# Starting the expert loop of a routed feed-forward layer on tables of the first half of the tokens

## The chip, the core and the metric

The kernel runs on one core of a Trainium2 chip. The metric is the time of one execution on the device, in microseconds (us). A core has five engines with their own instruction streams: TensorE (PE in the profile; PEld is its weight load), VectorE (DVE), ScalarE (ACT), GpSimd (POOL) and SyncE (SP), which here only starts transfers. Engines wait for each other through semaphores; each engine works its own stream strictly in the order written.

## What is computed

The reference is a stack of six sub-layers over 4096 tokens of width 128: routed feed-forward, causal attention, routed feed-forward again with the same weights, a second feed-forward, a two-branch attention, the second feed-forward again. Only the routed one matters here. It is computed twice, as `x = x + 0.5 * ffn(layernorm(x))` with

```python
logits = jnp.einsum('blh,he->ble', x, Wr) + br
top_expert = jnp.argmax(logits, axis=-1)
mask = jax.nn.one_hot(top_expert, 4, dtype=x.dtype)
for e in range(4):
    h1 = jax.nn.relu(jnp.einsum('blh,hf->blf', x, We1[e]) + be1[e])   # 128 -> 512
    oe = jnp.einsum('blf,fh->blh', h1, We2[e]) + be2[e]               # 512 -> 128
    out = out + mask[..., e:e + 1] * oe
```

So each token needs one expert of four.

## The kernel before, in words

`route_experts` is one such sub-layer; it is called with n = 0 (call 1, at the start of the kernel) and n = 1 (call 2, after the causal attention). It has two phases.

Routing. The 4096 tokens are 32 tiles of 128, in G = 8 groups of 4. DVE walks a software pipeline over steps s = 0 to 10: `statistics(s)`, `locate(s - 3)`, `scales(s)`, `choose(s - 2)`. ACT normalises, PE transposes a group (`turn`), computes its logits (`route`), and, once `choose` has made the one-hot mask, counts the ranks of the tokens within their experts (`tally`, into one of two halves of the PSUM tile `pos`, by the parity of the group). `locate` turns ranks into row numbers (`place`). POOL then scatters the normalised rows, one indirect transfer per tile of 128 tokens (32 per call), into a table in HBM, `routed_rows`, which has one region per expert. This is called the input scatter below.

Expert loop. The rows of each expert are cut into tiles of 128; at most SLOTS0 = 32 + 4 - 1 = 35 tiles (slots) occur. After the last group DVE computes from the final counts a table `tab`: for each slot its first row in `routed_rows` and the offset of its expert's weights. SP writes zero rows (`pad`) behind the end of each expert's rows, waits for the table, the pads and all 32 scatters (`sent`), and then loads the 35 row tiles into a ring of R = 12 buffers. For each slot PE transposes the rows (`turn_row`), ACT and DVE split them into two f16 parts (`high_x`, `low_x`), DVE copies the expert's weights into a ring of 6 buffers (`weights`), PE computes the hidden layer (`hidden`, 16 matmuls), ACT and DVE split the result (`relu`, `low`), PE computes the output (`output`, 13 matmuls), ACT copies it to a ring of S buffers (`result`), and POOL scatters it back to its tokens' places (the output scatter, 35 per call). POOL's queue has the output scatters behind the input scatters. A load into a buffer of the row ring waits until the output scatter of the slot 12 before has returned; `result` waits for the scatter S slots before.

In call 1 the weights come in f32 and are split into f16 parts on the way: `start.high` on ACT, `start.low` on DVE. Pairs 0 and 1 and the bias belong to this sub-layer; pairs 2, 3 and 4 belong to the second feed-forward layer, which runs much later.

Of the kernel before, what the change touches and what calls it, by code (L numbers as in the profile page):

```python
# [11 lines left out]
ALU = mybir.AluOpType  # L12
ACT = mybir.ActivationFunctionType
AX = mybir.AxisListType

P = 128
# [3 lines left out]
NT = TOK // P  # L20
# [5 lines left out]
E0, F0 = 4, 512  # L26
# [10 lines left out]
REGION = TOK + P  # L37
SLOTS0 = NT + E0 - 1
PADS = E0 + SLOTS0 - NT
ROWS = E0 * REGION + (SLOTS0 - NT) * P  # L40
REC = D + 1
FW = 5 * F0 + D
# [407 lines left out]
def route_experts(nc, tag, X, XNT, ident, rank, w, weights_in, consts, f0w, rows_d, y_d, tab, sent, returned, n,  # L450
                  start=None, ident_in=None):


    G = 8
    GT = NT // G
    wr, br, pick, tri, base, first, steps, numbers = (*w, *consts)
    R, S, W = 12, len(returned), 6
    with ExitStack() as ctx:
# [25 lines left out]
        expert = m.sb("expert", [P, SLOTS0])  # L484
        ones = m.sb("ones", [P, P], BF16)
# [32 lines left out]
        with nc.Block() as block:  # L518

            @block.vector  # L520
            def _(dve):
# [59 lines left out]

                for s in range(G + 3):
# [11 lines left out]
                link = Chain(dve, table)  # L594
# [4 lines left out]
                link(nc.vector.tensor_copy(ends[:, 0:1], tiles_of[:, 0:1]))  # L599
                for e in range(1, E0):  # L600
                    link(nc.vector.tensor_tensor(ends[:, e:e + 1], ends[:, e - 1:e], tiles_of[:, e:e + 1], ALU.add))
                link(nc.vector.tensor_scalar(jump[:], tiles_of[:], -float(P), float(REGION), ALU.mult, ALU.add))
                link(nc.vector.tensor_tensor(past[:], numbers[:].unsqueeze(2).broadcast_to([P, SLOTS0, E0]),
                                             ends[:].unsqueeze(1).broadcast_to([P, SLOTS0, E0]), ALU.is_ge))
                link(nc.vector.tensor_tensor(shift[:], past[:], jump[:].unsqueeze(1).broadcast_to([P, SLOTS0, E0]),
                                             ALU.mult))
                link(nc.vector.tensor_reduce(row[:], shift[:], AX.X, ALU.add))
                link(nc.vector.tensor_reduce(expert[:], past[:, :, 0:E0 - 1], AX.X, ALU.add))
                nc.vector.scalar_tensor_tensor(tab[:, 0, :], numbers[:], float(P), row[:], ALU.mult, ALU.add)\
                    .then_inc(tab_ready, 1)  # L610
                nc.vector.tensor_scalar(tab[:, 1, :], expert[:], float(FW), None, ALU.mult).then_inc(tab_ready, 1)
                dve.wait_ge(tab_ready, 2)
# [70 lines left out]
            @block.sync  # L683
            def _(sp):
                if start:
                    start.load(sp)
                sp.wait_ge(pad_ready, 2)
                sp.dma_start(rows_d[E0 * REGION:, :].rearrange("(i p) c -> p i c", p=P), pad[:, E0:, :])\
                    .then_inc(sent_spare, 16)
                sp.wait_ge(pads_placed, 1)  # L690
                for e in range(E0):
                    tail = sp.value_load(pad_row[0:1, e:e + 1], min_val=0, max_val=E0 * REGION - P)
                    sp.dma_start(rows_d[bass.ds(tail, P), :], pad[:, e, :]).then_inc(sent_spare, 16)
# [4 lines left out]
                for j in range(SLOTS0):  # L698
                    row = sp.value_load(tab[0:1, 0, j:j + 1], min_val=0, max_val=ROWS - P)
# [70 lines left out]
            def _(pe):  # L770
# [18 lines left out]
                def tally(c):  # L789
# [4 lines left out]
                    wide = GT + 1 if c == G - 1 else GT  # L794
# [1407 lines left out]
def program(nc, x, out, w, stop=99):  # L2202
# [6 lines left out]
    with ExitStack() as ctx:  # L2209
# [9 lines left out]
        loaded, cleared, sent, masks_in = (m.sem(n) for n in ("loaded", "cleared", "sent", "masks_in"))  # L2219
        pair_in, head_in = ([m.sem(f"{n}_in{r}") for r in range(RING)] for n in ("pair", "head"))  # L2220
        returned = [m.sem(f"returned{r}") for r in range(4)]
# [127 lines left out]
```

## Time and profile before

| what | value |
|---|---|
| median of 3 runs | 2858.43 us (2857.81 to 2858.5) |
| the profiled execution, whole | 2857.02 us |
| its span in the trace | 2855.3 us |
| PE, DVE, ACT, POOL busy over the span | 86%, 85%, 80%, 70% |
| granted TensorE clock, mean | 0.944 |
| call 1 of `route_experts` in the trace | about 0 to 144 us |
| call 2 | about 700 to 836 us |

The shares are means over the whole kernel, most of which is attention; what the change is worth is read from the two calls alone. Times in the trace are counted from the span's start.

### The profile page before, as it was taken

How to read it: one execution, taken by the hardware profiler on the slowest of the kernel's cores; microseconds unless marked ns; L12 is line 12 of the kernel's file. 1: busy time of each engine (PE TensorE's matmuls, PEld its weight loads, DVE VectorE, ACT ScalarE, POOL GpSimd, SP SyncE). 2: the span in 40 equal slices, each digit the busy share in tenths (PEclk: the TensorE clock that was granted, in tenths of full speed). 3: DMA queues.
4: the chain of work that ended last, by engine and by line, in shares of the span. 5: the costliest groups of instructions: out<-in, count | busy, mean ns of one | idle time of the engine just before them, and what ended most of it. 6: DMA issues, size and time to landing. Idle time of an engine off the chain costs nothing. (4 is left out here: it accounts for less than half of the span.)

```text
span 2855.3 us, 60213 instructions
## 1 busy us (share of the span) xinstructions
PE 2462.5 (86%) x18614; PEld 1012.2 (35%) x18614; DVE 2416.7 (85%) x3884; ACT 2294.2 (80%) x2640; POOL 2005.6 (70%) x1263
## 2 busy tenths in 40 slices
PE   4848999997669986999999999999999999986898
PEld 3823333334665652222222222222222222224566
DVE  6778888884666657999999999999999999996765
ACT  4655777776466546899999999999999999996654
POOL 5541222222644556799999999999999999994555
PEclk9978999999688997899999999999999999996899
DMA  5241100000220002000000000000000000000000
GB/s 145 63 127 33 29 28 28 28 29 4 63 68 1 1 1 102 16 18 15 14 14 15 15 17 15 14 14 15 15 17 15 14 14 15 15 5 1 1 12 19
DMA packets 96688, 76.58 MB, mean 27 GB/s; under 512 B 32592, under 2 KB 78168, under 8 KB 96448
## 3 DMA queue, kind: packets, MB, share of 16 engines
q1 hardware_dynamic: 92288, 66.36, 8.1%
q0 software_dynamic: 4288, 8.82, 0.9%
q8 instruction: 58, 0.95, 0.1%
q14 instruction: 54, 0.44, 0.1%
HBM read 47.77 MB, written 24.42 MB: 25 GB/s over the span
## 5 line engine op out<-in xcount | busy, mean ns | idle before, releaser
L1956 POOL TENSOR_TENSOR a_sg<-a_sg,all_f0w 128x1568 f32<-128x1568 f32 x256 | 904.9, 3535 | 21.3
L2099 ACT ACTIVATE a_pt<-a_pb 128x1024 f32<-128x1024 f32 x512 | 709.1, 1385 | 11.4 <-PE a_pb L2006 11.4
L2174 DVE TENSOR_REDUCE a_mx<-a_pm 128x1 f32<-128x1024 f32 x507 | 614.2, 1211 | 11.2 <-PE a_pm L2006 9.7
L2185 DVE TENSOR_SCALAR a_sg<-a_pa 128x1024 int32<-128x1024 int32 x512 | 616.1, 1203 | 8.0 <-PE a_pa L2006 7.8
L2108 ACT ACTIVATE a_sg<-a_sg,a_parh 128x2048 f32<-128x2048 f32 x256 | 605.4, 2365 | 15.3 <-POOL a_sg L1956 15.3
L2024 PE MATMUL a_po<-a_pt,a_Vh 128*32 128x512 f32 x2048 | 540.1, 605 | 65.1 <-ACT a_osb L2118 62.9
L2112 ACT ACTIVATE a_sg<-a_sg 128x2048 f32<-128x2048 f32 x256 | 584.4, 2283 | 0.1
L2024 PE MATMUL a_po<-a_sg,a_Vh 128*32 128x512 f32 x2048 | 539.8, 606 | 0.0
L1953 POOL TENSOR_SCALAR all_f0w<-a_sg,a_parh 128x1568 f32<-128x1568 f32 x256 | 513.9, 2008 | 28.9 <-DVE a_sg L2185 26.1
L1766 ACT ACTIVATE a_pt<-a_ring 128x1024 f32<-128x1024 f32 (+2 forms) x384 | 313.6, 846 | 150.3 <-PE a_ring L1693 146.9
L1838 DVE TENSOR_REDUCE a_mx<-a_ring 128x2 f32<-128x1024 f32 (+3 forms) x384 | 359.2, 956 | 73.6 <-PE a_ring L1676 54.7
L1607 POOL TENSOR_SCALAR_AFFINE_SELECT a_pt<-a_pt 128x256 f32<-128x256 f32 x256 | 104.0, 406 | 354.7 <-ACT a_pt L1766 354.4
L2006 PE MATMUL a_pm<-all_K,all_Q 96*128 96x512 bf16 x1014 | 312.2, 390 | 43.7 <-DVE a_mx L2174 33.4
L2006 PE MATMUL a_pb<-all_Q,all_K 128*128 128x512 bf16 x1024 | 309.1, 383 | 14.7 <-ACT a_pt L2099 11.6
L2006 PE MATMUL a_pa<-all_Q,all_K 96*128 96x512 bf16 x1024 | 310.7, 385 | 10.2 <-DVE a_sg L2185 1.2
L2192 DVE SCALAR_TENSOR_TENSOR a_sg<-a_sg,a_parh 128x480 f32<-128x480 f32 x256 | 218.3, 853 | 10.6
L2006 PEld LDWEIGHTS a_pm<-all_K,all_Q 96*128 96x128 bf16 x1014 | 63.1, 98 | 426.7 <-DVE a_mx L2174 362.0
L1040 ACT ACTIVATE f_sg<-f_psg 128x512 f32<-128x512 f32 x176 | 104.5, 594 | 116.0 <-PE f_psg L999 116.0
L1710 PE MATMUL a_po<-a_pt,a_Vh 128*32 128x384 f32 (+3 forms) x1920 | 191.2, 436 | 1.9 <-POOL a_pt L1607 1.8
L2024 PEld LDWEIGHTS a_po<-a_pt,a_Vh 128*32 128x32 f32 x2048 | 75.9, 108 | 280.4 <-issue 260.6
L1094 DVE TENSOR_TENSOR f_su<-f_psu,f_sg 128x512 f32<-128x512 f32 x144 | 98.7, 688 | 78.2 <-PE f_psu L999 73.3
L1693 PE MATMUL a_ring<-all_Q,all_K 50*128 50x512 bf16 (+2 forms) x768 | 132.1, 342 | 37.9 <-DVE a_mx L1838 32.7
(290 smaller groups left out, 4616.6 us busy)
## 6 DMA issues: line engine op xcount, KB each, us to landing
all_Q<-q_parts SPq DMA_DIRECT2D x256, 48.0 KB
all_K<-k_parts SPq DMA_DIRECT2D x256, 48.0 KB
k_parts<-p_parts SPq DMA_DIRECT2D x16, 384.0 KB, 2.8
e_recs<-routed_rows SPq DMA_DIRECT2D x70, 64.5 KB, 1.8
all_XNT<-expert_rows SPq DMA_DIRECT2D x16, 256.0 KB, 5.0
all_Q<-a_rows SPq DMA_DIRECT2D x256, 2.0 KB
q_parts<-p_parts SPq DMA_DIRECT2D x16, 192.0 KB, 2.4
q_parts<-p_parts SPq DMA_DIRECT2D x8, 384.0 KB, 2.6
```

Of the source, the lines that this page charges most:

```text
L1766: nc.scalar.activation(pt[n % 4][:, :, ga:gb, c * P:CH], of_weight(y)[:, :, 0:(gb - ga) * width].rearrange("p u (g n) -> p u g n", n=width ...
L1838: nc.vector.tensor_reduce(mx[:, j % 2, half, :, strip_at(t)], of_maximum(y)[:, :, 0:min(CH, (t + 1) * P - half * CH)], AX.X, ALU.max).then ...
L1953: nc.gpsimd.tensor_scalar(sums, buf[:, :, 0:CUT], b2, 1.0, ALU.add, ALU.mult)\
L1956: nc.gpsimd.tensor_tensor(buf[:, :, 0:CUT], buf[:, :, 0:CUT], sums, ALU.mult)\
L2006: last = nc.tensor.matmul(out[:, lo:lo + CH], lhsT[0:rows_, t * P:(t + 1) * P], rhs[0:rows_, lo:lo + CH], start=True, stop=True)
L2024: last = nc.tensor.matmul(po[32 * q:32 * q + 32, :], values, wts[:, i, half * CH:(half + 1) * CH], start=(t == 0), stop=(t == TT - 1))
L2099: nc.scalar.activation(pt[(j - LT) % 4][:, i, :], pb[:], ACT.Exp, scale=SC)\
L2108: nc.scalar.activation(buf[:], buf[:], ACT.Ln, bias=parh[:, ring(j, le), 1:2]).then_inc(ln_done, 1)
L2112: nc.scalar.activation(buf[:], buf[:], ACT.Exp, scale=-1.0).then_inc(sig_done, 1)
L2174: nc.vector.tensor_reduce(mx[:, (j // PER) % 2, t:t + 1], top[:], AX.X, ALU.max)\
L2185: nc.vector.tensor_scalar(sg[(j - ls) % 4][:, i, :].bitcast(I32), pa[:].bitcast(I32), SIGN_OFF, None, ALU.bitwise_and).then_inc(abs_done, 1)
L2192: nc.vector.scalar_tensor_tensor(buf[:, :, CUT:T], buf[:, :, CUT:T], parh[:, ring(j, ls), 0:1], buf[:, :, CUT:T], ALU.add, ALU.mult).then_ ...
```

## The change

After group 3 of a call, the first half of the tokens (16 tiles) has its ranks. `tally(3)` now also sums the counts (one more column group), and DVE computes a first table from them at step s = 7: for each expert the number of full tiles of first-half tokens. Four experts leave at most three tiles short, so at least 16 - 3 = 13 tiles are full; slots 0 to 12 of the table (EARLY0 = 13) are these. `tally(5)`, which overwrites the counts, waits for the table's first instruction. The semaphore `sent` is split in two halves; SP starts to load rows when the first table is there and the first 16 scatters have landed. Its pads move behind the twelfth load, and ahead of slot 13 it waits for the second table and the second 16 scatters. The second table (slots 13 to 34) is still computed at the end of routing, ahead of the expert loop, and has four more instructions. The ring of output buffers grows from 4 to 6. `start.low` of pairs 2 to 4 moves behind the expert loop.

```diff
+HALF_NT = NT // 2
+EARLY0 = HALF_NT - E0 + 1
...
+                def spread(count, slots, at):
+                    link(nc.vector.tensor_tensor(past[:, 0:slots, :],
+                                                 numbers[:, 0:slots].unsqueeze(2).broadcast_to([P, slots, E0]),
+                                                 count[:].unsqueeze(1).broadcast_to([P, slots, E0]), ALU.is_ge))
...
+                def first_table():
+                    link(nc.vector.tensor_tensor(held[:], ranked(G // 2 - 1)[:, GT, :], first[:], ALU.subtract))
+                    link(nc.vector.tensor_tensor(more[:, :, 0:HALF_NT],
+                                                 held[:].unsqueeze(2).broadcast_to([P, E0, HALF_NT]),
+                                                 steps[:, 1:HALF_NT + 1].unsqueeze(1).broadcast_to([P, E0, HALF_NT]),
+                                                 ALU.is_ge))
+                    link(nc.vector.tensor_reduce(full[:], more[:, :, 0:HALF_NT], AX.X, ALU.add))
+                    summed(full_ends, full)
+                    link(nc.vector.tensor_scalar(taken[:], full_ends[:], float(EARLY0), None, ALU.min))
+                    link(nc.vector.tensor_scalar(jump[:], full[:], -float(P), float(REGION), ALU.mult, ALU.add))
+                    spread(full_ends, EARLY0, 0)
+                    nc.vector.scalar_tensor_tensor(tab[:, 0, 0:EARLY0], numbers[:, 0:EARLY0], float(P),
+                                                   row[:, 0:EARLY0], ALU.mult, ALU.add).then_inc(tab_ready, 1)
...
                     if 0 <= s - 2 < G:
                         choose(s - 2)
+                    if s == G // 2 + 3:
+                        first_table()
...
-                dve.wait_ge(tab_ready, 2)
+                link(nc.vector.tensor_tensor(ends[:], ends[:], taken[:], ALU.subtract))
...
+                dve.wait_ge(tab_ready, 4)
...
                 weights(0)
                 weights(1)
-                for i in range(2, len(start.pairs) if start else 0):
-                    start.low(dve, i)
                 for s in stages:
...
                     if inside(s - 1):
                         low(s - 1)
+                for i in range(2, len(start.pairs) if start else 0):
+                    start.low(dve, i)
...
-                            .then_inc(sent, 16)
+                            .then_inc(sent[k // HALF_NT], 16)
...
-                sp.wait_ge(pads_placed, 1)
...
                 sp.wait_ge(tab_ready, 2)
-                sp.wait_ge(sent_spare, 16 * (1 + E0))
-                sp.wait_ge(sent, 16 * NT * (n + 1))
+                sp.wait_ge(sent[0], 16 * HALF_NT * (n + 1))
                 for j in range(SLOTS0):
+                    if j == R:
+                        sp.wait_ge(pads_placed, 1)
...
+                    if j == EARLY0:
+                        sp.wait_ge(tab_ready, 4)
+                        sp.wait_ge(sent_spare, 16 * (1 + E0))
+                        sp.wait_ge(sent[1], 16 * HALF_NT * (n + 1))
...
+                    if c == G // 2 + 1:
+                        pe.wait_ge(table, 1)
-                    wide = GT + 1 if c == G - 1 else GT
+                    wide = GT + 1 if c in (G // 2 - 1, G - 1) else GT
...
-        returned = [m.sem(f"returned{r}") for r in range(4)]
+        returned = [m.sem(f"returned{r}") for r in range(6)]
```

DVE's stream at step 7 of call 1, before the change, from the last instruction of `choose(5)` (the mask) on: `locate(5)` and the start of `choose(6)` follow.

```order
L566 TENSOR_TENSOR e_mask<-e_pref,e_top 128x16
L578 TENSOR_TENSOR e_eq<-e_pos,e_mask 128x16
L580 TENSOR_REDUCE e_place<-e_eq 128x4
L558 TENSOR_TENSOR e_score<-e_psr,all_br 128x16
L560 TENSOR_REDUCE e_top<-e_score 128x4
```

The same place after the change; L573 is the mask of `choose(5)`, and the rows behind it are the first table (lines have moved by some 7 to 40 numbers).

```order
L573 TENSOR_TENSOR e_mask<-e_pref,e_top 128x16
L610 TENSOR_TENSOR e_held<-e_pos,all_plan 128x4
L611 TENSOR_TENSOR e_more<-e_held,all_plan 128x4x16
L615 TENSOR_REDUCE e_full<-e_more 128x4
L604 COPY e_fullends<-e_full 128x1
L606 TENSOR_TENSOR e_fullends<-e_fullends,e_full 128x1 x3
L617 TENSOR_SCALAR e_taken<-e_fullends 128x4
L618 TENSOR_SCALAR e_jump<-e_full 128x4
L593 TENSOR_TENSOR e_past<-all_plan,e_fullends 128x52
L596 TENSOR_TENSOR e_shift<-e_past,e_jump 128x52
L598 TENSOR_REDUCE e_row<-e_shift 128x13
L599 TENSOR_REDUCE e_expert<-e_past 128x13
```

Two writes of `all_tab` (128x13) follow, and then `locate(5)`: fifteen instructions have come in ahead of it.

SP's stream in call 1 before the change, from the last pad to the first row load, with the semaphores it waits for:

```order
L692 TENSOR_LOAD e_padrow
L692 ISA x2
L693 ISA
L693 DMA routed_rows<-e_pad 128x129
L699 TENSOR_LOAD all_tab [waits all_sent,e0_sentspare,e0_tabready]
L699 ISA x2
L703 ISA
L703 DMA e_recs<-routed_rows 128x129
```

After the change the first row load stands ahead of all pads (L743 waits for `sent0` and the first table alone); twelve loads on, this piece follows, from the last pad to the load of slot 13:

```order
L738 DMA routed_rows<-e_pad 128x129
L743 TENSOR_LOAD all_tab
L743 ISA x2
L747 ISA [waits all_returned0,e0_rturned]
L747 DMA e_recs<-routed_rows 128x129
L743 TENSOR_LOAD all_tab [waits all_sent1,e0_sentspare,e0_tabready]
L743 ISA x2
L747 ISA [waits all_returned1,e0_rturned]
L747 DMA e_recs<-routed_rows 128x129
```

The wait for the whole scatter has moved from slot 0 to slot 13, behind a load (slot 12) that waits for the return of slot 0's output scatter.

DVE's stream at the end of call 1 after the change (before it, the block ended behind the last `e_hidl`):

```order
L665 TENSOR_TENSOR e_xl<-e_pt,e_xh 128x128
L673 TENSOR_TENSOR e_hidl<-e_hid,e_hidh 128x512 x2
L442 SCALAR_TENSOR_TENSOR all_wgl<-all_Q,all_wgh 128x1408
L442 SCALAR_TENSOR_TENSOR all_wul<-all_Q,all_wuh 128x1408
L442 SCALAR_TENSOR_TENSOR all_wdl<-all_K,all_wdh 128x1408
L525 UNCONDITIONAL_BRANCH
```

The three splits for the second feed-forward layer now stand here; before, they stood between the second weight copy and the first `e_xl`.

## Rows read from the trace of the kernel before

**Rows 1.** Waits of call 1, 64 to 140 us: total us, times, longest us.

```profile
PE e_pt L826 <- DMA e_recs<-routed_rows: 24.6, 2, 23.6
```

**Rows 2.** Waits of call 2, 756 to 830 us.

```profile
PE e_pt L826 <- DMA e_recs<-routed_rows: 18.7, 2, 18.0
```

**Rows 3.** Timeline of POOL, call 1: start, duration, instruction, idle before.

```profile
36.05 0.96 POOL L670 DMA_INDIRECT routed_rows<-e_rec,e_place  x1 [0.31 <-issue]
...
47.42 2.88 POOL L670 DMA_INDIRECT routed_rows<-e_rec,e_place  x1 [0.31 <-issue]
...
58.46 1.23 POOL L670 DMA_INDIRECT routed_rows<-e_rec,e_place  x1 [0.31 <-issue]
...
61.53 1.23 POOL L670 DMA_INDIRECT routed_rows<-e_rec,e_place  x1 [0.30 <-issue]
75.98 1.22 POOL L677 DMA_INDIRECT expert_rows<-e_ysb,e_recs  x1 [13.23 <-ACT e_ysb L758]
...
135.41 0.96 POOL L677 DMA_INDIRECT expert_rows<-e_ysb,e_recs  x1 [0.31 <-issue]
```

**Rows 4.** Timeline of SP and what it starts: first row loads of both calls, next stage.

```profile
64.92 6.37 SPq L703 DMA_DIRECT2D e_recs<-routed_rows  x6
...
755.80 18.38 SPq L703 DMA_DIRECT2D e_recs<-routed_rows  x15
...
144.25 5.52 SPq L1197 DMA_DIRECT2D all_XNT<-expert_rows  x8
```

**Rows 5.** Timeline of PE, call 1: first row transpose, first hidden matmul.

```profile
66.93 0.45 PE L826 MATMUL e_pt<-all_ident,e_recs 128*128 128x128 f32 x1 [23.65 <-DMA e_recs<-routed_rows]
...
68.63 0.32 PE L838 MATMUL e_pt<-e_xh,e_slot 128*128 128x128 f16 x1
```

**Rows 6.** Timeline of DVE, call 1.

```profile
34.06 0.17 DVE L566 TENSOR_TENSOR e_mask<-e_pref,e_top 128x16 bf16<-128x16 f32 x1
...
36.89 0.17 DVE L558 TENSOR_TENSOR e_score<-e_psr,all_br 128x16 f32<-128x16 f32 x1 [1.25 <-PE e_psr L786]
...
43.68 0.15 DVE L593 CAST e_padrow<-e_pos 128x4 int32<-128x4 f32 x1
...
47.18 4.49 DVE L440 SCALAR_TENSOR_TENSOR all_f0w<-all_V,all_f0w 128x2048 f16<-128x2048 f32 x2
...
55.65 1.69 DVE L618 COPY e_slot<-all_f0w 128x2688 f16 x2 [1.12 <-issue]
57.25 1.60 DVE L440 SCALAR_TENSOR_TENSOR all_wgl<-all_Q,all_wgh 128x1408 f16<-128x1408 f32 x1
...
132.05 0.69 DVE L633 TENSOR_TENSOR e_hidl<-e_hid,e_hidh 128x512 f16<-128x512 f32 x1 [0.94 <-ACT e_hid L751]
```

**Rows 7.** Timeline of POOL, call 2.

```profile
746.40 0.96 POOL L670 DMA_INDIRECT routed_rows<-e_rec,e_place  x1 [0.30 <-issue]
...
752.72 0.96 POOL L670 DMA_INDIRECT routed_rows<-e_rec,e_place  x1 [0.30 <-issue]
767.14 1.38 POOL L677 DMA_INDIRECT expert_rows<-e_ysb,e_recs  x1 [13.47 <-ACT e_ysb L758]
...
827.11 0.96 POOL L677 DMA_INDIRECT expert_rows<-e_ysb,e_recs  x1 [0.31 <-issue]
```

**Rows 8.** Timeline of DVE, call 2.

```profile
744.35 1.63 DVE L618 COPY e_slot<-all_f0w 128x2688 f16 x2 [0.79 <-DVE all_tab L611]
758.49 0.29 DVE L625 TENSOR_TENSOR e_xl<-e_pt,e_xh 128x128 f16<-128x128 f32 x1 [12.51 <-ACT e_xh L741]
```

**Rows 9.** Timeline of PE, call 2: first hidden matmul.

```profile
759.09 0.32 PE L838 MATMUL e_pt<-e_xh,e_slot 128*128 128x128 f16 x1
```

**Rows 10.** Stretches of call 2: length, busy us of PE, PEld, DVE, ACT, POOL, clock, DMA.

```profile
761.00:765.00 4.00, 3.80 (x36) 3.53 (x35) 2.91 (x6) 2.51 (x6) 0.00 (x0) 0.52 0.27 66
765.00:770.00 5.00, 4.89 (x84) 4.65 (x82) 4.21 (x8) 3.98 (x12) 2.50 (x2) 1.00 0.26 70
```

More of the change, by code:

```diff
@@ L484, in route_experts @@
         expert = m.sb("expert", [P, SLOTS0])
+        full = m.sb("full", [P, E0])
+        full_ends = m.sb("fullends", [P, E0])
+        taken = m.sb("taken", [P, E0])
+        moved = m.sb("moved", [P, E0])
+        origin = m.sb("origin", [P, 1])
         ones = m.sb("ones", [P, P], BF16)
@@ L580, in locate @@
                     nc.vector.tensor_reduce(place[:, t], eq[:, t, :], AX.X, ALU.max).then_inc(placed, 1)
+                link = Chain(dve, table)
+                def spread(count, slots, at):
+                    link(nc.vector.tensor_tensor(past[:, 0:slots, :],
+                                                 numbers[:, 0:slots].unsqueeze(2).broadcast_to([P, slots, E0]),
+                                                 count[:].unsqueeze(1).broadcast_to([P, slots, E0]), ALU.is_ge))
+                    link(nc.vector.tensor_tensor(shift[:, 0:slots, :], past[:, 0:slots, :],
+                                                 jump[:].unsqueeze(1).broadcast_to([P, slots, E0]), ALU.mult))
+                    link(nc.vector.tensor_reduce(row[:, 0:slots], shift[:, 0:slots, :], AX.X, ALU.add))
+                    link(nc.vector.tensor_reduce(expert[:, 0:slots], past[:, 0:slots, 0:E0 - 1], AX.X, ALU.add))
+                    nc.vector.tensor_scalar(tab[:, 1, at:at + slots], expert[:, 0:slots], float(FW), None, ALU.mult)\
+                        .then_inc(tab_ready, 1)
@@ new lines, in summed @@
+                def summed(out, counts):
+                    link(nc.vector.tensor_copy(out[:, 0:1], counts[:, 0:1]))
+                    for e in range(1, E0):
+                        link(nc.vector.tensor_tensor(out[:, e:e + 1], out[:, e - 1:e], counts[:, e:e + 1], ALU.add))
+                def first_table():
[11 more added lines that the diff above has]
+                                                   row[:, 0:EARLY0], ALU.mult, ALU.add).then_inc(tab_ready, 1)
@@ L590, in _ @@
                         choose(s - 2)
+                    if s == G // 2 + 3:
+                        first_table()
                 ahead = ranked(G - 1)[:, GT, :]
                 nc.vector.tensor_copy(pad_row[:], ahead).then_inc(pads_placed, 1)
-                link = Chain(dve, table)
                 link(nc.vector.tensor_tensor(held[:], ahead, first[:], ALU.subtract))
@@ L598, in _ @@
                 link(nc.vector.tensor_reduce(tiles_of[:], more[:], AX.X, ALU.add))
-                link(nc.vector.tensor_copy(ends[:, 0:1], tiles_of[:, 0:1]))
-                for e in range(1, E0):
-                    link(nc.vector.tensor_tensor(ends[:, e:e + 1], ends[:, e - 1:e], tiles_of[:, e:e + 1], ALU.add))
+                summed(ends, tiles_of)
+                link(nc.vector.tensor_tensor(ends[:], ends[:], taken[:], ALU.subtract))
                 link(nc.vector.tensor_scalar(jump[:], tiles_of[:], -float(P), float(REGION), ALU.mult, ALU.add))
[L603 to L611, printed above, removed]
-                dve.wait_ge(tab_ready, 2)
+                link(nc.vector.tensor_tensor(moved[:, 0:E0 - 1], taken[:, 1:], taken[:, 0:E0 - 1], ALU.subtract))
+                link(nc.vector.scalar_tensor_tensor(jump[:, 0:E0 - 1], moved[:, 0:E0 - 1], float(P), jump[:, 0:E0 - 1],
+                                                    ALU.mult, ALU.add))
+                link(nc.vector.tensor_scalar(origin[:], taken[:, 0:1], float(P), None, ALU.mult))
+                late = SLOTS0 - EARLY0
+                spread(ends, late, EARLY0)
+                nc.vector.scalar_tensor_tensor(tab[:, 0, EARLY0:], row[:, 0:late], origin[:], steps[:, 0:late],
+                                               ALU.add, ALU.add).then_inc(tab_ready, 1)
+                dve.wait_ge(tab_ready, 4)
                 def weights(j):
@@ L689, in _ @@
                     .then_inc(sent_spare, 16)
-                sp.wait_ge(pads_placed, 1)
-                for e in range(E0):
-                    tail = sp.value_load(pad_row[0:1, e:e + 1], min_val=0, max_val=E0 * REGION - P)
-                    sp.dma_start(rows_d[bass.ds(tail, P), :], pad[:, e, :]).then_inc(sent_spare, 16)
                 sp.wait_ge(tab_ready, 2)
-                sp.wait_ge(sent_spare, 16 * (1 + E0))
-                sp.wait_ge(sent, 16 * NT * (n + 1))
+                sp.wait_ge(sent[0], 16 * HALF_NT * (n + 1))
                 for j in range(SLOTS0):
+                    if j == R:
+                        sp.wait_ge(pads_placed, 1)
+                        for e in range(E0):
+                            tail = sp.value_load(pad_row[0:1, e:e + 1], min_val=0, max_val=E0 * REGION - P)
+                            sp.dma_start(rows_d[bass.ds(tail, P), :], pad[:, e, :]).then_inc(sent_spare, 16)
+                    if j == EARLY0:
+                        sp.wait_ge(tab_ready, 4)
+                        sp.wait_ge(sent_spare, 16 * (1 + E0))
+                        sp.wait_ge(sent[1], 16 * HALF_NT * (n + 1))
                     row = sp.value_load(tab[0:1, 0, j:j + 1], min_val=0, max_val=ROWS - P)
@@ L2218, in program @@
         stacks = [m.sb(n, [P, 2 * RING, T], BF16) for n in ("Q", "K")]
-        loaded, cleared, sent, masks_in = (m.sem(n) for n in ("loaded", "cleared", "sent", "masks_in"))
+        loaded, cleared, masks_in = (m.sem(n) for n in ("loaded", "cleared", "masks_in"))
+        sent = [m.sem(f"sent{i}") for i in range(2)]
         pair_in, head_in = ([m.sem(f"{n}_in{r}") for r in range(RING)] for n in ("pair", "head"))
-        returned = [m.sem(f"returned{r}") for r in range(4)]
+        returned = [m.sem(f"returned{r}") for r in range(6)]
         layer = {n: {k[3:]: v for k, v in w.items() if k.startswith(n)} for n in ("f0_", "a0_", "a1_", "f1_")}
```

## The prediction

> **What bounds the kernel now.** The change touches two stretches of some 140 us, so I read those and leave the rest of the span alone. First the waits of each call: PE's longest one, once routing is over, is for the first rows of the expert loop, 23.6 us in call 1 [rows 1] and 18.0 us in call 2 [rows 2]. Then POOL's timeline says why these rows are late: input scatters go out 1.26 us apart (0.96 and 0.30 idle), the last starts at 61.53 in call 1 [rows 3] and at 752.72 in call 2 [rows 7], and SP's first load starts 2.16 and 2.12 us after these end [rows 4]. That is the landing time of a scatter. Then DVE: in call 2 its first weight copies are done by 746 and it stands idle for 12.51 us until the first row is there [rows 8]; in call 1 it is ready only after 57.25, since the weight split stands in between [rows 6]. So what ends last ahead of the loop is the scatter, with DVE next: about 10 us behind it in call 1, about 12 in call 2. From the first hidden matmul (68.63 and 759.09 [rows 5, 9]) to the start of the last output scatter (135.41 and 827.11 [rows 3, 7]) the loop takes 66.8 and 68.0 us, a train of 35 slots of some 1.75 us (the output scatters of call 1 are (135.41 - 75.98) / 34 = 1.75 apart). PE is busy in 4.89 of 5 us there [rows 10]. A loop that starts earlier and keeps its pace ends as much earlier.
>
> **The rows are early enough.** The sixteenth scatter of call 1 starts at 36.05, ends at 37.01 and lands some 2.16 later, at 39.2. The first table is done by 37.3 (below). SP's loads go out 6.37 / 6 = 1.06 us apart, and the first arrives 66.93 - 64.92 = 2.0 us after its start [rows 4, 5]: rows 0 and 1 are there at 41.2 and 42.3, all twelve by 53. In call 2 the sixteenth scatter is 16 x 1.26 us ahead of the one at 752.72, at 732.6 [rows 7]; it lands at 735.7, against a first weight copy at 744.35 [rows 8]. The whole first wait goes; what is late next is DVE.
>
> **DVE, first table.** Before, the 15 instructions from L593 to the end of the table take 47.18 - 43.68 = 3.5 us [rows 6], with operands of up to 140 elements. The first table has 15 too, with at most 64; at 0.2 us for a small one and its wait this is 3.0 at least, 3.5 at most; I take 3.1. It starts where the mask of group 5 ends, at 34.06 + 0.17 = 34.2, and ends at 37.3. DVE waits there for PE anyway: it starts `choose(6)`, two instructions of `locate` later, at 36.89 after an idle 1.25. Now it starts it at 37.3 + 0.3 = 37.6, and from there on PE and DVE take turns as before: 0.7 us later. The bounds are 0 (all of it in the idle time) and 3.1 (none). What waits behind it on DVE are `locate(5)` to `locate(7)`; POOL needs their rows only from the twenty-first scatter on, at 36.05 + 5 x 1.26 = 42.4 [rows 3], so the scatter is not held up. `tally(5)` waits for the table's first instruction alone, 0.15 us behind the mask that it needs anyway.
>
> **DVE, second table.** Four more small instructions, 0.8 us, and narrower operands (22 slots instead of 35), which give back some 0.2: +0.6. With 0.7 this is 1.3 us for everything behind it on DVE.
>
> **The start of the loop.** Call 1: the first weight copy starts at 55.65 + 1.3 = 56.95, the second is over at 57.25 + 1.3 = 58.55; the three splits that stood there [rows 6] are gone, the first `e_xl` takes 0.29 [rows 8], and hidden starts at about 58.9 instead of 68.63: **9.7 us**. Call 2: copies from 744.35 + 1.3 = 745.65, over 1.6 later, e_xl, hidden at 747.6 instead of 759.09: **11.5 us**.
>
> **Is the loop held up later?** The first output scatter starts 75.98 - 68.63 = 7.35 us after the first hidden matmul in call 1 and 8.05 in call 2, thus now at 66.2 and 755.7. The input scatters ended at 62.8 and 753.7; beside DVE's weight copies they take 1.23 and 0.30 instead of 1.26 together (as 58.46 to 61.53 shows, 1.53 apart [rows 3]). Six are left in call 2 at 746.4: +1.6, end 755.3. POOL is free just in time in call 2 and early in call 1. The second half has landed at 64.9 and 757.4, the pads (four at the pace of loads, behind twelve loads) long before. The load of slot 12 waits for the return of output scatter 0: 755.7 + 1.4 + 2.1 = 759.2 in call 2, and its rows arrive at about 761. PE turns slot 12 some eleven slots after the first hidden matmul, about 747.6 + 2 + 11 x 1.75 = 769. A cover of 8 us. Six output buffers instead of four hold up ACT less, not more. Nothing is charged here.
>
> **The end of call 1.** The three splits now run from 132.05 + 0.69 = 132.7 (in the old time [rows 6]) beside the last three output scatters. The row beside the same splits has scatters 1.53 apart instead of 1.26, so the last one ends 0.8 later, or 1.5 if the first of them has to let a split pass; DVE itself ends 3 x 1.6 later, at 137.5, before the last scatter has landed (136.4 + 2.1). I charge **1.0 us**. From the last scatter to the next stage stay 144.25 - 135.41 = 8.84 us [rows 3, 4].
> A rule of the Trainium skill speaks against this place: SBUF — State Buffer, section "Who interferes with whom", says that a DVE instruction with two SBUF inputs and a GpSimd one that reads SBUF exclude each other for the whole instruction. The scatter of 2.88 us next to the longer split at 47.18 agrees; those next to the splits of 1.60 us slipped in between them. By the harshest reading, no scatter until all three are through, the end is 4 us late instead of 1, and the sum 17.2.
>
> **Sum.** 9.7 + 11.5 - 1.0 = 20.2 us. The profiled execution took 2857.02 (its span and 1.7 us around it), which gives 2836.8; the median of the runs is 1.41 above it, so the forecast is 2838.2, taken as **2838 us** (-0.71%). Bounds: DVE's delay by the first table, 0 to 3.1 in each call, gives +1.4 to -4.8 in all; the two loops differ in length by 1.2 us, so each may trade places with the other, +1.2 to -1.2; the tail +1.0 to -3.0. Together 23.8 to 11.2 us: 2834.6 to 2847.2.
>
> **Rivals.**
> 1. *POOL becomes the late one in call 2.* If each of the six scatters left takes 2.88 + 0.30 [rows 3] beside DVE's loop, the input scatter ends at 746.4 + 6 x 3.18 = 765.5, ten after the first output is ready. ACT's seventh result waits for the first return (769.0 against 766.1), the load of slot 12 likewise, and POOL makes up 0.2 us per slot (1.55 against 1.75). That costs some 4 us: 2842. For: the row with 2.88. Against: that was a split of 2.25 us, and all output scatters beside the loop's own copies took about 1.23.
> 2. *The change doesn't do what it says: the first sixteen scatters are seen to land only with the last.* Then SP starts as before, the loop too, and only the tail is paid: 2859. For: no row shows a landing in mid-stream. Against: the landing after the last is 2.1 us in both calls, so no backlog is left there, and DMA is at 0.27 of its time in the loop [rows 10].
> 3. *Slower: TensorE stays at its low level for more slots.* In 761 to 765 the granted clock is 0.52 and 36 matmuls pass in 4 us; in 765 to 770 it is 1.00 and 84 pass in 5 us [rows 10]. That is 0.111 against 0.060 us, 0.05 for each of 30 matmuls, 1.5 us per slot. The gain is eaten at 14 slots more at 1.2 GHz over both calls; with 18 more it is 2864. For: the loop starts in other surroundings, with DVE's copies beside POOL's scatters. Against: in both calls the idle ahead of the loop gets shorter, and the work per slot is as dense as before. The Trainium skill's TensorE: Matmul & The Clock Gate, section "What's actually happening", has the low level as the default that activity lifts; the trace agrees with the step from 0.52 to 1.00 at about 765.
>
> **Chances.** Forecast 0.78 (its own range 2834 to 2842), rival 1 0.12, rival 2 0.05, rival 3 0.03, something else 0.02. Within 0.2% (5.7 us, about what a measurement tells from no change) falls rival 2; faster are the forecast, rival 1 and half of the rest: 0.91, 0.05 and 0.04. The range 2833 to 2847 takes in the bounds and so the forecast and rival 1, and leaves out the rest.
>
> **What would show it.** In the changed profile: first row load near 39 in call 1; a first hidden matmul near 58.9, and in call 2 some 17 us after the mask of group 5; DVE's first copy as what it waits for, not the rows; no PE wait for rows at slot 12 or 13; last output scatter 66.8 and 68 us after the first hidden matmul; the three splits behind the last `e_hidl` with scatters about 1.5 apart. Wrong would be: a PE wait for rows in mid-loop, a first output scatter over 8 us behind the hidden matmul, or a longer loop.

## The result and the profile after

The changed kernel takes 2839.05 us (median of 4 runs, 2837.36 to 2840.34) against 2858.47 us of the kernel before (4 runs, 2857.81 to 2859.08): ratio 0.9932, 95% interval 0.9915 to 0.9949, 19.4 us faster. The forecast was 2838, with 2833 to 2847. The profiled execution of the changed kernel is the slowest of its four, 2840.34 us, with a span of 2838.6 us.

The waits of the changed kernel, call 1 (38 to 135 us) and call 2 (735 to 830 us): total us, times, longest us.

```profile
PE e_pt L884 <- DVE e_xl L665: 14.4, 1, 14.4
...
DVE e_slot L658 <- issue: 2.8, 8, 1.1
...
PEld e_pt L872 <- DMA e_recs<-routed_rows: 0.2, 1, 0.2
...
PE e_pt L884 <- DVE e_xl L665: 7.2, 1, 7.2
```

PE's waits of 23.6 and 18.0 us for rows [rows 1, 2] are gone; 0.2 us is left. What PE now waits for ahead of the loop is DVE's first `e_xl`, in both calls.

SP and what it starts in the changed kernel: first row loads and the next stage, call 1 and call 2.

```profile
40.36 13.40 SPq L747 DMA_DIRECT2D e_recs<-routed_rows  x12
...
136.95 3.56 SPq L1243 DMA_DIRECT2D all_XNT<-expert_rows  x6
...
730.06 13.63 SPq L747 DMA_DIRECT2D e_recs<-routed_rows  x12
...
818.44 4.74 SPq L135 DMA_DIRECT2D all_XNT<-expert_rows  x8
```

PE in the changed kernel: the first hidden matmul of both calls.

```profile
59.00 0.26 PE L884 MATMUL e_pt<-e_xh,e_slot 128*128 128x128 f16 x1 [14.35 <-DVE e_xl L665]
...
742.74 0.26 PE L884 MATMUL e_pt<-e_xh,e_slot 128*128 128x128 f16 x1 [7.20 <-DVE e_xl L665]
```

DVE in the changed kernel: first table, second table, splits and first weight copies of call 1, its last splits, the first instruction of call 2, and call 2's second weight copy.

```profile
34.23 0.15 DVE L610 TENSOR_TENSOR e_held<-e_pos,all_plan 128x4 f32<-128x4 f32 x1
...
37.26 0.17 DVE L585 TENSOR_TENSOR e_eq<-e_pos,e_mask 128x16 f32<-128x16 f32 x1
...
37.65 0.16 DVE L565 TENSOR_TENSOR e_score<-e_psr,all_br 128x16 f32<-128x16 f32 x1
...
44.39 0.15 DVE L636 CAST e_padrow<-e_pos 128x4 int32<-128x4 f32 x1
...
48.51 4.49 DVE L442 SCALAR_TENSOR_TENSOR all_f0w<-all_V,all_f0w 128x2048 f16<-128x2048 f32 x2
53.03 2.81 DVE L448 SCALAR_TENSOR_TENSOR all_f0w<-all_K,all_Q 1x2560 f16<-1x2560 f32 x1
56.97 1.68 DVE L658 COPY e_slot<-all_f0w 128x2688 f16 x2 [1.13 <-issue]
58.58 0.28 DVE L665 TENSOR_TENSOR e_xl<-e_pt,e_xh 128x128 f16<-128x128 f32 x1
...
123.56 1.62 DVE L442 SCALAR_TENSOR_TENSOR all_wgl<-all_Q,all_wgh 128x1408 f16<-128x1408 f32 x1
125.09 1.62 DVE L442 SCALAR_TENSOR_TENSOR all_wul<-all_Q,all_wuh 128x1408 f16<-128x1408 f32 x1
126.62 1.62 DVE L442 SCALAR_TENSOR_TENSOR all_wdl<-all_K,all_wdh 128x1408 f16<-128x1408 f32 x1
...
694.81 0.87 DVE L534 BATCH_NORM_STATS2 e_stats<-all_X 128x6 f32<-128x128 f32 x4 [0.65 <-PEq L80]
...
741.54 0.86 DVE L658 COPY e_slot<-all_f0w 128x2688 f16 x1 [0.35 <-issue]
```

In call 1 everything on DVE up to `e_xl` stands where it was forecast to within 0.1 us, and behind the second table DVE works without a gap but for 1.13 us ahead of the first copy (1.12 before [rows 6]).

POOL in the changed kernel: the last input scatter and the tail of call 1, then input and first output scatters of call 2, and its last output scatter.

```profile
61.72 0.96 POOL L710 DMA_INDIRECT routed_rows<-e_rec,e_place  x1 [0.30 <-issue]
...
123.78 2.23 POOL L717 DMA_INDIRECT expert_rows<-e_ysb,e_recs  x1 [0.66 <-ACT e_ysb L802]
126.31 1.23 POOL L717 DMA_INDIRECT expert_rows<-e_ysb,e_recs  x1 [0.30 <-issue]
127.84 1.23 POOL L717 DMA_INDIRECT expert_rows<-e_ysb,e_recs  x1 [0.30 <-issue]
...
740.61 1.91 POOL L710 DMA_INDIRECT routed_rows<-e_rec,e_place  x1 [0.31 <-issue]
742.82 1.63 POOL L710 DMA_INDIRECT routed_rows<-e_rec,e_place  x1 [0.30 <-issue]
...
750.01 1.31 POOL L710 DMA_INDIRECT routed_rows<-e_rec,e_place  x1 [0.30 <-issue]
751.63 1.01 POOL L717 DMA_INDIRECT expert_rows<-e_ysb,e_recs  x1 [0.30 <-issue]
...
809.57 0.96 POOL L717 DMA_INDIRECT expert_rows<-e_ysb,e_recs  x1 [0.30 <-DMA expert_rows<-e_ysb,e_recs]
```

**Where the time came from.** Call 2 has moved as a whole, so its marks are counted from its first DVE instruction: 700.04 before, 694.81 after. In call 1 the first hidden matmul comes 68.63 - 59.00 = 9.6 us earlier [rows 5], and the next stage 144.25 - 136.95 = 7.3 us [rows 4]. In call 2 it comes 59.05 - 47.93 = 11.1 us earlier, and the last output scatter 127.07 - 114.76 = 12.3 us [rows 7, 9]. Together that is 19.6 us. The profiled spans differ by less, 16.7 us: the stretch between the calls is 2.1 us longer in this profile and the one behind them 0.8 us. No instruction of these stretches was changed. Over the profiles of all kernels here the first varies from 555.2 to 560.4 us and the second from 2017.7 to 2023.3; the medians differ by 19.4.

### The profile page after: what moved, and what is told of

Its sections match the earlier page's. It is cut to its first block and busy times, and to the rows that moved or that the text cites. A ratio compares the mean times of both kernels' runs of the same rounds, so it can differ in the third digit from the quotient of the medians.

```text
span 2838.6 us, 60256 instructions
## 1 busy us (share of the span) xinstructions
PE 2463.7 (87%) x18616; PEld 1013.4 (36%) x18616; DVE 2423.2 (85%) x3922; ACT 2293.9 (81%) x2640; POOL 2009.1 (71%) x1263
## 5 line engine op out<-in xcount | busy, mean ns | idle before, releaser
L2145 ACT ACTIVATE a_pt<-a_pb 128x1024 f32<-128x1024 f32 x512 | 709.3, 1385 | 11.1 <-PE a_pb L2052 11.1
```

Source lines behind the costliest of these rows:

```text
L2145: nc.scalar.activation(pt[(j - LT) % 4][:, i, :], pb[:], ACT.Exp, scale=SC)\
```

## The experiments

Marks of every run: us at which the first hidden matmul and the next stage's first load start, in call 2 from the call's first DVE instruction, and the median of the runs. The kernel before was run again beside each group: 2858.3, 2857.1, 2856.8 and 2858.4.

| kernel | hidden 1 | next stage 1 | hidden 2 | next stage 2 | median |
|---|---|---|---|---|---|
| before | 68.63 | 144.25 | 59.05 | 135.95 | 2858.47 |
| changed | 59.00 | 136.95 | 47.93 | 123.63 | 2839.05 |
| changed, again (e9) | 58.97 | 136.61 | 47.93 | 123.65 | 2837.65 |
| wait for all scatters (e1) | 67.92 | 145.28 | 59.50 | 135.90 | 2858.36 |
| ring of 4 (e2) | 59.02 | 136.64 | 48.21 | 123.61 | 2841.07 |
| splits back (e3) | 63.60 | 140.00 | 47.94 | 123.66 | 2843.70 |
| no splits (e4) | 59.04 | 134.63 | 47.84 | 123.89 | 2837.36 |
| longer first table (e6) | 62.47 | 139.14 | 51.97 | 127.12 | 2844.96 |
| second table in the loop (e5) | 54.84 | 136.21 | 43.45 | 123.62 | 2836.34 |
| copies in gaps (e7) | 53.95 | 134.81 | 41.41 | 121.72 | 2834.97 |
| splits in gaps (e8) | 51.75 | 132.68 | 41.41 | 122.13 | 2833.49 |
| table in pieces (e10) | 54.91 | 138.85 | 43.23 | 125.48 | 2844.39 |
| pieces and gaps (e11) | 51.85 | 136.44 | 41.43 | 123.90 | 2839.20 |

**All scatters awaited (e1).** The tables, the ring and the moved splits stay; SP's wait and its pads go back ahead of the first load.

```diff
-                sp.wait_ge(tab_ready, 2)
-                sp.wait_ge(sent[0], 16 * HALF_NT * (n + 1))
+                sp.wait_ge(pads_placed, 1)
...
+                sp.wait_ge(tab_ready, 4)
+                sp.wait_ge(sent_spare, 16 * (1 + E0))
+                for i in range(2):
+                    sp.wait_ge(sent[i], 16 * HALF_NT * (n + 1))
...
```

> The changed kernel with one part undone: SP writes the pads first and waits for both tables and all 32 scatters ahead of slot 0, as before the change. First table, split semaphore, ring of six and the moved splits stay. Theory (the gain comes from not waiting for the second half of the scatter): the first hidden matmul is back at 68 to 69 us in call 1, PE waits for rows again, over 20 us, and the time is that of before plus what the late splits cost at the end of call 1: 2859 to 2862 us. Rival (the ring of six or the moved splits bring part of the gain): 2855 us or less.

The ratio to the kernel before is 0.9999 (0.999 to 1.0009), and PE waits for rows again, in call 1:

```profile
PE e_pt L869 <- DMA e_recs<-routed_rows: 23.3, 2, 22.3
```

So the gain hangs on the early start: without it, the rest of the change brings nothing beyond the interval of some 2.7 us either way. With it, the moved splits are worth 3 us of call 1's gain (e3).

**Ring of four buffers (e2).**

```diff
-        returned = [m.sem(f"returned{r}") for r in range(6)]
+        returned = [m.sem(f"returned{r}") for r in range(4)]
```

> The changed kernel with a ring of 4 output buffers, as before. Theory (POOL comes some 2.4 us late to the first output of call 2, and four slots of 1.75 us cover that): the same as the changed kernel within 2 us, 2837 to 2841. Rival (the ring of six is needed since POOL is still busy with the input scatter when outputs arrive): ACT's fifth result of call 2 waits for the first return, the loop of call 2 is longer by 2 us or more, 2842 or more.

Both calls end where they did (136.64 and 123.61). The median, 2841.07, has runs from 2836.86 to 2844.78, which hold the changed kernel's too; the marks settle it: the ring of six isn't needed.

**Splits back in front of the loop (e3).**

```diff
                 weights(1)
+                for i in range(2, len(start.pairs) if start else 0):
+                    start.low(dve, i)
                 for s in stages:
...
-                for i in range(2, len(start.pairs) if start else 0):
-                    start.low(dve, i)
```

> The changed kernel with the three splits for the second feed-forward layer back between the second weight copy and the first e_xl. Theory (DVE is what the loop's start now waits for): the first hidden matmul of call 1 comes 4.6 us later, at 63.6; the end of call 1 gets back 1.5 to 2 us, since the last scatters have no split beside them: +3 us on the changed kernel, 2842. Rival (something else, such as PE or the rows, sets the start of call 1): the first hidden matmul stays near 59, and the time falls by 1.5 to 2 us, to 2837.

DVE in this kernel, call 1: the first of the three splits, and the first `e_xl` behind them.

```profile
58.57 1.61 DVE L442 SCALAR_TENSOR_TENSOR all_wgl<-all_Q,all_wgh 128x1408 f16<-128x1408 f32 x1
...
63.17 0.28 DVE L665 TENSOR_TENSOR e_xl<-e_pt,e_xh 128x128 f16<-128x128 f32 x1
```

The first hidden matmul comes 4.6 us later, as long as DVE works on the three splits (58.57 to 63.17), and call 1 ends 3.05 us later. SP loads the rows from 39.6 us on, as in the changed kernel; so it is DVE that the start waits for. Call 2, which has no splits, is unchanged.

**No splits at all (e4).** The low parts of the second feed-forward layer's weights are zeros, written by ACT.

```diff
+        if i >= 2:
+            self.nc.scalar.activation(self.pairs[i][3], home, ACT.Copy, scale=0.0)
...
-                for i in range(2, len(start.pairs) if start else 0):
-                    start.low(dve, i)
```

> The changed kernel with the three late splits left out: ACT writes zeros into the low parts of the second feed-forward layer's weights instead, in its idle time ahead of the loop, so that layer computes with the high parts alone. This measures the end of call 1 by itself. Theory (the splits hold up the last three output scatters by 1.5 to 2 us): from the last output split of DVE to the next stage call 1 is 1.5 to 2 us shorter than in the changed kernel, scatters 1.26 us apart: 2837. Rival (the splits cost the 1.0 us charged, or nothing): 0 to 1.0 us shorter. Rival (the harshest reading of the port rule): 4 us shorter.

POOL in this kernel, the last three output scatters of call 1:

```profile
123.28 0.96 POOL L717 DMA_INDIRECT expert_rows<-e_ysb,e_recs  x1 [0.66 <-ACT e_ysb L802]
124.54 0.96 POOL L717 DMA_INDIRECT expert_rows<-e_ysb,e_recs  x1 [0.30 <-ACT e_ysb L802]
125.80 0.96 POOL L717 DMA_INDIRECT expert_rows<-e_ysb,e_recs  x1 [0.30 <-DMA expert_rows<-e_ysb,e_recs]
```

From the start of the first of the three to the end of the last it takes 3.48 us; with the splits beside it 5.29 (123.78 to 129.07). So the splits cost 1.8 us in the scatters. The next stage starts 2.0 to 2.3 us earlier than in the two profiles of the changed kernel.

**A longer first table (e6).** Fifteen small instructions more in the chain.

```diff
+                    for _ in range(15):
+                        link(nc.vector.tensor_scalar(moved[:], taken[:], 1.0, None, ALU.mult))
```

> The changed kernel with the first table made longer by 15 small chained DVE instructions that nothing reads (3.0 us). Theory (the first table has used up DVE's idle time in routing, and DVE is what the loop waits for): the first hidden matmul comes 2.9 us later in both calls (61.9, and 50.8 us after the start of call 2), and the time grows by 5.8 us, to 2845. Rival (the three waits of DVE for PE that are left in routing, 1.1 to 1.3 us each, still cover it): less than 1 us later in each call, 2841 or less.

The fifteen instructions take 3.7 us in each call, not the 3.0 that was expected of them. Hidden starts 3.5 and 4.0 us later, the calls end 2.2 and 3.5 us later, and the time is 2844.96. DVE has next to no cover left in front of the loop.

**Second table inside the loop (e5).** DVE computes it in slot 1, ahead of the first `low`.

```diff
...
-                dve.wait_ge(tab_ready, 4)
...
+                dve.wait_ge(tab_ready, 2)
...
                     if inside(s + 2):
+                        if s + 2 == EARLY0:
+                            dve.wait_ge(tab_ready, 4)
                         weights(s + 2)
+                    if s == 1:
+                        second_table()
                     if inside(s - 1):
                         low(s - 1)
```

> The changed kernel with the second table moved from ahead of the loop into it: behind the fourth weight copy, ahead of the first e_hidl; the first copies wait for the first table alone. Theory (DVE is what the start of the loop waits for, and it stands idle 1.5 us ahead of the first e_hidl): the first hidden matmul comes 4 us earlier in both calls (55 us, and 43.9 us after the start of call 2 instead of 47.9), the first e_hidl 2.6 us later behind it, and each call ends 1.3 us or a little more earlier: about 3 us off the changed kernel, 2836. Rival (PE sets the loop, DVE has room in it): each call ends 4 us earlier, 2831. Rival (DVE sets the whole loop, so the table costs the same wherever it stands): no change, 2839.

A miss: the start comes 4.2 and 4.5 us earlier, the end only 0.7 and 0.0. PE's windows, first 10 us behind the first hidden matmul of call 2, of this kernel (length, busy us of PE, PEld, DVE, ACT, POOL, clock, DMA share, GB/s):

```profile
736.60:746.60 10.00, 7.47 (x67) 7.08 (x68) 8.48 (x28) 3.80 (x9) 8.11 (x7) 0.50 0.41 108
```

and of the changed kernel, with most of its loop in call 1 as the second row:

```profile
742.70:752.70 10.00, 9.76 (x131) 9.30 (x132) 8.05 (x15) 6.37 (x17) 8.29 (x6) 0.78 0.28 81
...
64.00:120.00 56.00, 55.42 (x941) 54.34 (x940) 51.22 (x93) 44.24 (x125) 37.07 (x30) 1.00 0.22 64
```

67 matmuls instead of 131. PE stands idle for 2.5 us ahead of the third slot's hidden matmul, which by the kernel's text needs the third `e_xl`; in DVE's stream this stands behind the table and the first `e_hidl`, and it ends at 742.90. Rows of PE and of DVE in this kernel:

```profile
743.11 0.27 PE L891 MATMUL e_pt<-e_xh,e_slot 128*128 128x128 f16 x1 [2.53 <-issue]
```

```profile
742.01 0.68 DVE L676 TENSOR_TENSOR e_hidl<-e_hid,e_hidh 128x512 f16<-128x512 f32 x1
742.62 0.28 DVE L668 TENSOR_TENSOR e_xl<-e_pt,e_xh 128x128 f16<-128x128 f32 x1
```

The granted clock stays at 0.50, the 1.2 GHz level, over the whole window of 10 us.

**DVE's gaps filled (e7, e8).** On top of e5: in call 2 the first two weight copies stand in DVE's two last waits of routing, in call 1 the reads of their offsets (e7); then, in call 1, the two long splits stand there instead, the reads of the offsets go back behind routing, and ACT makes the first high part one step earlier (e8). The middle of the step from e7 to e8:

```diff
...
                     if s in (G, G + 1):
-                        offset(s - G)
-                        if not start:
+                        if start:
+                            start.low(dve, s - G)
+                        else:
+                            offset(s - G)
                             copy(s - G)
...
```

> The kernel with the late second table, and the expert offsets of slots 0 and 1 read during DVE's last two waits in routing; in call 2 their weight copies stand there too. Theory (DVE sets the start): the first hidden matmul of call 1 is 1.1 us earlier than with the late table alone (53.8), that of call 2 some 2 us (about 42 us after its start); POOL, whose input scatter ends at about 56 us of call 2, is then some 7 us late to the first output, just under what six buffers carry (10.5 us less the scatter's 3.1): 2 to 3 us off that kernel, about 2833. Rival (POOL is now the bound in call 2: ACT waits for the return of the first output scatter): call 2 ends no earlier than with the late table alone, 2835 or more.

> The kernel with the copies in the gaps, and in call 1 DVE's two long weight splits (2.25 us each) moved from behind routing into its last waits there, behind choose(6) and choose(7); ACT makes the first high part one step earlier, in its own wait. Theory (DVE's busy time sets the end of a call, so what is put into its idle time is won): 2.3 us of the first split and 1.3 us of the second vanish in the waits; call 1 ends 3 to 3.5 us earlier than with the copies in the gaps alone (at 131.5 instead of 134.8), call 2 the same: 2832. Rival (PE or POOL takes over as the bound of call 1): call 1 ends less than 1 us earlier, 2834 to 2835.

e7 ends the calls 1.4 and 1.9 us earlier than e5; the medians, 2834.97 (some 2833 was expected) and 2836.34, don't tell them apart, the marks do. e8 ends call 1 another 2.1 us earlier, where 3 to 3.5 were expected. The shortfall lies ahead of the loop: the first hidden matmul comes 2.2 us earlier, and from it to the last output scatter the loop takes 71.8 us in both kernels. A new idle stretch of DVE, 1.39 us, makes it up; it stands behind the two reads of the offsets, which were in routing's waits in e7. POOL's scatters get longer beside the splits and copies, but the loop is no longer for it. The rows:

```profile
46.72 2.81 DVE L448 SCALAR_TENSOR_TENSOR all_f0w<-all_K,all_Q 1x2560 f16<-1x2560 f32 x1 [1.39 <-issue]
...
47.38 3.37 POOL L732 DMA_INDIRECT routed_rows<-e_rec,e_place  x1 [0.30 <-issue]
...
65.07 1.05 POOL L739 DMA_INDIRECT expert_rows<-e_ysb,e_recs  x1 [0.31 <-issue]
```

POOL's input scatters now last till 64.8, right up to its first output scatter. e8 has the lowest median: 2833.49 us, ratio to before 0.9921 (0.9906 to 0.9935), against 2837.65 us of the changed kernel beside it.

**The changed kernel again (e9).**

> The changed kernel once more, beside the one above, for the size of its effect and of what varies: 2839 within 2 us; the ends of the two calls as in its first profile within 0.5 us (137.0, and 123.6 us after the start of call 2), while the stretches between and behind the calls, which the change does not touch, differ by up to 2 us each.

2837.65 us, ratio 0.9933 (0.9919 to 0.9947). Both calls end within 0.4 us of their first profile. The stretch between the calls is 2.6 us longer than there, more than the 2 us that were expected.

**The table in pieces (e10, e11).** Nine pieces, one behind each of the first nine `low`, in e5 and in e8.

```diff
...
-                    if s == 1:
-                        second_table()
                     if inside(s - 1):
                         low(s - 1)
+                    if s >= 1:
+                        next(pieces, None)
```

> The kernel with the second table inside the loop (the run before of that kind), but the table cut into nine pieces of 0.2 to 0.8 us, one behind each of the low parts of slots 0 to 8, instead of 4.1 us in one piece ahead of the first. Two theories of why an earlier start of 4.2 and 4.5 us ended only 0.7 and 0.0 us earlier there. Theory A, TensorE: the table in one piece made it wait 3.1 and 3.0 us in the second slot, and after that it stayed at its low level till 10.6 and 11.7 us behind the first hidden matmul, instead of 5.4 and 4.4: 66 to 70 matmuls in the first 10 us instead of 125 to 132. In pieces that wait is gone, the full pace comes at 4 to 6 us, and the calls end some 3 us earlier: next stage near 133 us in call 1, 120.5 us behind the call's start in call 2, some 2830 us in all. Theory B, DVE: its work from the end of routing on sets the loop's end wherever the table stands in it; then both ends stay at 136.2 and 123.6, and the time at 2836.

> The same cut of the second table in the kernel that also fills DVE's waits of the routing with offsets, copies and two weight splits (2833.5 us, next stage at 132.7 and 122.1). Theory A, TensorE's wait and low level: both ends some 2.5 to 3.5 us earlier, near 129.7 and 119, and some 2828 us. Theory B, DVE's work: no change, 2833 us. If POOL, whose first output scatter was pushed to 65.1 us there, is what holds call 1, call 1 stays at 132.7 and only call 2 gains.

Neither theory expected this: both kernels end later than with the table in one piece, by 2.6 and 1.9 us (e10 against e5) and 3.8 and 1.8 us (e11 against e8). DVE of e10, call 1, the weight copies around the first pieces:

```profile
59.85 0.86 DVE L670 COPY e_slot<-all_f0w 128x2688 f16 x1 [0.44 <-issue]
...
62.27 0.86 DVE L670 COPY e_slot<-all_f0w 128x2688 f16 x1 [0.44 <-issue]
...
65.15 0.89 DVE L670 COPY e_slot<-all_f0w 128x2688 f16 x1 [0.45 <-issue]
...
79.96 0.85 DVE L670 COPY e_slot<-all_f0w 128x2688 f16 x1
```

The eight slots between them take 79.96 - 59.85 = 20.1 us, 2.5 each instead of 1.75, in all the 6 us by which this loop is longer than that of the changed kernel (74.85 against 68.84 from first hidden matmul to last output scatter). DVE has little room there, as the second of the changed kernel's windows above shows: it works 51.22 of 56 us (and PE 55.42). A piece adds its own length (3.9 us for all nine in call 1, 0.43 on average) and, all but the last, an idle 0.44 to 0.72 us ahead of the weight copy.

So cutting the table brought a cost of its own, and these runs don't decide between the theories for the table in one piece. In call 1 of e10 TensorE reached its full pace as early as theory A wants (4.7 us behind the first hidden matmul), and the loop was still longer. In call 2 it didn't: for 8.4 us behind the first hidden matmul the granted clock is 0.50, with 69 matmuls. What e10 and e11 show is that the pieces cost DVE time which the slots around them can't take up. How the loss of e5 divides between DVE's work on the table and TensorE's wait with its longer stay at the low level was not separated. Nor was it tried to read the copy's address ahead of a piece.

## Why the prediction was right, step by step

- **The rows are early enough: right.** SP's first load starts at 40.36, forecast 39.2: the sixteenth scatter ended at 37.04 and the load followed 3.3 us later, not 2.16. In e9 the same load starts at 39.53. This is covered either way, since DVE's first `e_xl` comes 18 us later. It also rules out rival 2: the load starts 21 us ahead of the last input scatter (61.72).
- **DVE's tables: right.** The first takes 37.26 - 34.23 = 3.0 us (forecast 3.1), `choose(6)` starts at 37.65 (37.6), and the first copy at 56.97 (56.95). e3 (4.6 us for 4.6) and e6 (3.5 and 4.0 for 3.7) show that a microsecond more on DVE is about a microsecond more ahead of the loop.
- **The start of the loop: right.** Call 1 9.6 us (9.7), call 2 11.1 (11.5). Call 2's 0.4 us is an idle 0.35 us of DVE between its two weight copies (741.54), which ran without a gap before [rows 8].
- **Is the loop held up later: right that it costs nothing, but closer than told.** In call 2 five of the six input scatters beside DVE's copies took 1.31 to 1.91 us and one 0.96, where 1.23 was forecast, and the last started at 750.01. The price was read from the wrong neighbour: next to the scatters from 58.46 to 61.53 [rows 3] DVE worked on the splits [rows 6], not on weight copies. POOL took the first result at 751.63, some 2.3 us after ACT had it; from 759 on its idle time ahead of a scatter was above 0.30 us again, so it had caught up. This is rival 1 in a mild form. No wait of PE for rows came back at slot 12.
- **The end of call 1: too small.** Charged 1.0 us, measured 1.8 in the scatters and 2.0 to 2.3 at the next stage. The second of the two cases that the prediction named, 1.5 us if the first scatter has to let a split pass, is nearer to what came. The first scatter was held up by 1.27 us by a split (2.23 instead of 0.96, e4), and each of the others took 0.27 more. By the harshest reading of the rule cited there (the Trainium skill, SBUF — State Buffer, section "Who interferes with whom") no scatter would have passed till the splits ended at 128.24; the trace doesn't agree: two start at 126.31 and 127.84, beside them. Read for one DVE instruction at a time the rule fits: the splits end at 125.18, 126.71 and 128.24, and each scatter ends 0.83 us behind the split that ran when it started, at 126.01, 127.54 and 129.07. So the scatters beside the splits of 1.60 us didn't slip in between them, as the prediction has it; each waited for one.
- **Keeps its pace: right here, not in general.** In call 2 the loop took 66.83 us instead of 68.02 [rows 7, 9], 1.2 us gained, as the bounds allowed. About half of that is TensorE's: counted by matmuls, its full pace came 4.4 us behind the first hidden matmul, not 5.8, and 1.4 us less at 0.111 us a matmul instead of 0.060 [rows 10] is worth 0.6 us; where the rest came from wasn't followed. Rival 3 is out by the same count: it needs 14 slots more at the low level, and in call 1 the full pace came 5.4 us behind (4.4 before, and 4.4 in e9). e5 shows the limit: a start made earlier by moving DVE's work into the loop is mostly lost again there. (In rival 3, 18 slots at 1.5 us make 2865, not 2864; nothing hangs on it.)
- **The sum.** Charged 20.2; the two calls give 7.3 + 12.3 = 19.6, and the medians 19.4. The mechanism was right, and that the sum is this close is partly luck: the tail of call 1 cost some 1 us more than charged and call 2's start gained 0.4 less, while call 2's loop gained 1.2 for which nothing was entered.

What stays open: why the stretch between the calls varies by 5 us. In 200 to 300 us the mean granted clock is 0.81 to 0.85, in 600 to 700 us 0.94 to 1.00 in the profiles compared; that this is all of it wasn't shown.

## What to carry to other kernels

When a transfer that is awaited ends last, find out what ends next, and by how much: here that was DVE, 10 to 12 us behind, and this distance was the gain. Work for a loop's later part may start early if its inputs are complete, but an engine that works over nine tenths of the loop is no place to put its preparation: fill that engine's waits ahead of the loop first. If something must go into the loop, price each cut as well: here one piece was cheaper than nine. Price what a moved piece does to its new neighbours by the nearest row in which the two already ran side by side, and make sure that the row's neighbour is the one you mean.

## What the runs showed of the hardware that was not expected

- An indirect scatter beside DVE's splits and copies takes 1.01 to 3.37 us instead of 0.96 on POOL, and its end hangs on DVE's instruction: beside the splits at the end of call 1 it came 0.83 us behind the end of a split each time (rows above). Beside weight copies it comes 0.12 or 0.83 us behind the end of a copy: the scatter of 740.61 ends at 742.52, the copy of 741.54 at 742.40. In seven of the profiles nearly all scatters of over 1.0 us around the loops' starts and at call 1's end come out so. The scatter of 2.88 us in the kernel before [rows 3] does, too: it ends at 50.30, and the first of the two splits, at half of their 4.49 us [rows 6], at 49.42. What a moved scatter will take can be estimated from this, by where in DVE's instruction it starts.
- In e10 DVE was idle for 0.44 to 0.72 us ahead of eight of the nine weight copies that had a piece of the table before them, and at most 0.23 us ahead of the five copies after those. The copy's source address is read from a table, and this read may be what waits; that was not tested. In the waits of call 1 the idle time is 2.8 us in the changed kernel and 5.9 us in e10:

```profile
DVE e_slot L670 <- issue: 5.9, 13, 1.1
```

- TensorE's low pace isn't always seen in the granted clock. In the changed kernel, windows with the columns as above:

```profile
59.00:64.00 5.00, 4.80 (x43) 4.47 (x44) 3.34 (x6) 2.44 (x6) 3.07 (x3) 1.00 0.14 44
...
742.70:747.00 4.30, 4.06 (x36) 3.76 (x37) 2.75 (x6) 1.69 (x4) 3.57 (x3) 0.50 0.34 96
```

Both have one matmul in 0.12 us, but the clock reads 1.00 in the first and 0.50 in the second. The count of matmuls told the pace.
